# Two expert branches recomputed with features on partitions and 512 tokens as columns

## The chip, the cores and the metric

The kernel runs on one NeuronCore of a Trainium2 chip. The metric is the device time of the whole program in microseconds (us). Engines: PE is TensorE (matmul), DVE is VectorE, ACT is ScalarE, POOL is GpSimd, SP is SyncE, which here only issues DMAs.

## The reference, cut to what matters

x has 2 batches of 2048 tokens with 256 features. Two layers follow each other; each computes `x = x + s * silu(...)`, with s an attention output. The change lies in the feed-forward part of layer 0, whose two branches (forward and inverse, 8 experts of rank 64 each) are

```
xV = einsum('btd,kdr->btkr', Q_side, V)           # 8 experts x 64 per branch
yW = einsum('btd,kdr->btkr', K_side, W)
prod = xV * cumsum(yW, axis=1)
weights = softmax(gelu(Q_side @ router_w1.T + b1) @ router_w2.T + b2 + expert_bias)
out = einsum('btkr,kdr->btd', prod * weights[..., None], U) + weights @ b
out = out / n_valid                                # 1, 2, 3, ... along the sequence
g = silu((fwd + alpha * inv) @ W_O.T)
x1 = x + (attention @ W_o.T + b_o + xn) * g
```

Both branches together have 2 * 8 * 64 = 1024 columns per token. Float32 precision is kept by splitting operands into a high part of a shorter type (fp32r) and the rest, and by three products (high*high, high*rest, rest*high).

## The kernel before, in words

The program is a chain of phases with a barrier between them: weights, projection of layer 0, full attention, combination with the experts (`phase_combine_experts`, here called the stage), then projection, banded attention and combination of layer 1. The folded weights AQ, BK (256 x 1024), UO (1024 x 256) and bO are made once in the weights phase; the softmaxed router weights, already divided by n_valid, lie in SBUF as `logits`, tokens on partitions. The projection has left the transposed normed input (xT) and its running sum (cT) in DRAM, high part and rest.

The stage works on 32 tiles of 128 tokens, four to a chunk of 512 tokens, chunks in the order batch 0, batch 1, batch 0, ... For each tile, tokens lie on partitions:

- `front` (L1743 to L1759): ps_xv[128 x 1024] = xT.T @ AQ and ps_cy[128 x 1024] = cT.T @ BK, each 2 x 6 matmuls (`split_matmul`, L66 to L73) of 512 columns.
- ACT copies ps_xv to SBUF (L1822), DVE multiplies with ps_cy (L1861), POOL multiplies by the router weights (L1898).
- `turn` (L1761 to L1777): TensorE transposes the tile of attention outputs (2 transposes), of router weights (1) and of the weighted products (8, into ps_pt). ACT copies the high parts (L1811 to L1816), DVE makes the rests (L1849 to L1854).
- `out` (L1779 to L1789): 6 matmuls of 256 columns with o0, 24 with UO, and the plain float32 product with bO (2 records in the trace).
- ACT takes the tanh (L1828), DVE makes the gate (`gate_steps`, L1941 and L1943), POOL multiplies and adds to x (`residual`, L1950 and L1952).

The order on TensorE is turn(n), front(n + 1), out(n). So the router and split steps of one tile have a whole front of the next to finish in. SP loads chunk by chunk, two buffers (one a batch); one semaphore per buffer counts all 14 loads of a chunk (turned operands, x, xn and four pieces of attention), and front waits for the whole of it (L1747). The batches of 8 tiles run in a hardware loop of 3 turns with one more copy behind it.

Of the kernel before, what the change touches and what calls it, by code (L numbers as in the profile page):

```python
# [23 lines left out]
F32 = mybir.dt.float32  # L24
# [1621 lines left out]
def load_att(sp, S, att, loaded, i, u):  # L1646

    for hg in range(NG2):
        slot = (u * NG2 + hg) * NCH + i + 1
        sp.dma_start(att[:, u, :, hg * G * C:(hg + 1) * G * C],  # L1650
                     S["att"][ds(slot, 1)].rearrange("o (a p) c -> p (o a) c", p=P)).then_inc(loaded, DMA)


def store_and_load(sp, passed, x1_done, stored, x_io, out_dram, load):

    def store(i, u):
        wait_apart(sp, x1_done, 2 + TILES_BODY * i + TT * (u + 1), passed)
        sp.dma_start(out_dram[u, ds(i * CH, CH), :].rearrange("(t p) d -> p t d", p=P), x_io[:, u]
                     ).then_inc(stored[u], DMA)

    load(0, 0)
    load(0, 1)
    with sp.Fori(0, NCH - 1) as i:
        for u in range(2):
            store(i, u)
            wait_apart(sp, stored[u], DMA * (i + 1), passed)
            load(i + 1, u)
    for u in range(2):
        store(NCH - 1, u)
    for u in range(2):  # L1670
        wait_apart(sp, stored[u], DMA * NCH, passed)


def phase_combine_experts(nc, W, S, x_dram, out_dram):


    with ExitStack() as ctx:
        n_ = Names(nc, ctx, "c0")
        x_io = n_.sb("x_io", [P, 2, TT, D])
        xn = n_.sb("xn", [P, 2, TT, D])  # L1680
        att = n_.sb("att", [P, 2, TT, D])
        xT = n_.sb("xT", [P, 2, 2, DK, CH], F32R)
        cT = n_.sb("cT", [P, 2, 2, DK, CH], F32R)
        xv = n_.sb("xv", [P, 2 * KR])
        prod = n_.sb("prod", [P, 2 * KR])
        wprod = n_.sb("wprod", [P, 2 * KR])
        pT = n_.sb("pT", [P, 2, 2 * KR], F32R)
        aT = n_.sb("aT", [P, 2, D], F32R)
        wT = n_.sb("wT", [2 * E, P])
        wtile = n_.sb("wtile", [P, TILES_BODY, 2 * E])  # L1690
        sums = n_.sb("sums", [P, 2, D])
        eg = n_.sb("eg", [P, D])
# [3 lines left out]
        ps_pt = n_.ps("ps_pt", 2 * CH)  # L1696
        ps_out = n_.ps("ps_out", CH)
        ps_m = n_.ps("ps_m", CH)

        passed = n_.sem("passed")  # L1700
        loaded = [n_.sem(f"loaded{u}") for u in range(2)]
        stored = [n_.sem(f"stored{u}") for u in range(2)]
        xv_ready = n_.sem("xv_ready")
        cy_ready = n_.sem("cy_ready")
        xv_copied = n_.sem("xv_copied")
        prod_done = n_.sem("prod_done")
        wprod_done = n_.sem("wprod_done")
        m_ready = n_.sem("m_ready")
        pt_ready = n_.sem("pt_ready")
        high = n_.sem("high")  # L1710
        low = n_.sem("low")
# [5 lines left out]
        wtile_done = n_.sem("wtile_done")  # L1717
# [4 lines left out]
        n_loads = 4 * DK + 2 + NG2  # L1722

        order = [(u, t) for u in range(2) for t in range(TT)]

        @block.sync
        def _(sp):
            def load(i, u):
                tok = ds(i * CH, CH)
                for part in range(2):  # L1730
                    for k in range(DK):
                        sp.dma_start(f32(xT[:, u, part, k, :]), S["xT"][u, part, k, :, tok]).then_inc(loaded[u], DMA)
                        sp.dma_start(f32(cT[:, u, part, k, :]), S["cT"][u, part, k, :, tok]).then_inc(loaded[u], DMA)
                rows = lambda x: x[u, tok, :].rearrange("(t p) d -> p t d", p=P)
                sp.dma_start(x_io[:, u], rows(x_dram)).then_inc(loaded[u], DMA)
                sp.dma_start(xn[:, u], rows(S["xn"])).then_inc(loaded[u], DMA)
                load_att(sp, S, att, loaded[u], i, u)

            store_and_load(sp, passed, x1_done, stored, x_io, out_dram, load)
# [555 lines left out]
```

## Time and profile before

| | us |
|---|---|
| median of 3 runs | 2621.84 (2611.28 to 2631.97) |
| the profiled execution, device time | 2636.41 |
| its span, first to last instruction | 2634.8 |
| PE busy | 2305.5 (88% of the span) |
| DVE, ACT, POOL busy | 1831.5, 1466.2, 442.8 |

The span is what lies between the first and the last instruction of the profiled execution; 1.6 us lie around it. Busy times are of the whole program; the stage in question is one part of it, from about 1716 us to 2099 us after the start of the span. PEld is the load of the stationary operand, which can run beside the matmul before it; its start times tell well how fast TensorE moves on, since the ends of matmuls are modelled.

### The profile page before, as it was taken

To read this page: it belongs to the slowest core of one execution; us is meant where nothing else is said; L and a number is where in the kernel's file an instruction comes from. 1 tells how busy PE (TensorE), PEld (TensorE's weight loads), DVE (VectorE), ACT (ScalarE), POOL (GpSimd) and SP (SyncE) were. 2 spreads that over 40 slices of the span, in tenths; PEclk is the share of its full clock that TensorE was granted. 3 is DMA by queue.
4 is the path that set the end of the run, shared out by engine and by line. 5 is a ranking of instruction groups with operands and counts; after the bars stand their busy time and mean duration, and the time that the engine had idled before them with its cause. 6 is when DMAs were issued, how large, how long until landed. Compare 5 with 4: busy or idle time off the path is not lost. (4 is left out here: it accounts for less than half of the span.)

```text
span 2634.8 us, 45348 instructions
## 1 busy us (share of the span) xinstructions
PE 2305.5 (88%) x15192; PEld 1296.4 (49%) x15192; DVE 1831.5 (70%) x3165; ACT 1466.2 (56%) x2211; POOL 442.8 (17%) x647
## 2 busy tenths in 40 slices
PE   4678499999999999999999999769999775799988
PEld 2456133333333333333333333258888664566568
DVE  2654789999999999999999999113333364768836
ACT  2343067777777777777777777712222231346543
POOL 0000000000000000000000000023333300346545
PEclk9799589999999999999999999979999987658799
DMA  3786900220400404004022000033323089856465
GB/s 116 240 274 236 132 3 5 43 29 7 65 3 19 53 5 64 8 11 61 3 43 31 7 17 3 7 112 83 109 77 114 33 299 306 147 120 155 110 174 161
DMA packets 204953, 229.59 MB, mean 87 GB/s; under 512 B 72576, under 2 KB 143104, under 8 KB 200896
## 3 DMA queue, kind: packets, MB, share of 16 engines
q1 hardware_dynamic: 191920, 208.63, 31.9%
q10 hardware_dynamic: 7152, 13.84, 2.8%
q0 software_dynamic: 5728, 5.00, 0.8%
q8 instruction: 107, 1.75, 0.3%
q14 instruction: 46, 0.38, 0.1%
HBM read 129.28 MB, written 96.73 MB: 86 GB/s over the span
## 5 line engine op out<-in xcount | busy, mean ns | idle before, releaser
L930 DVE TENSOR_REDUCE a_maxes<-a_ps_a 128x2 f32<-128x1024 f32 x1024 | 1202.7, 1221 | 117.6 <-PE a_ps_a L1043 112.7
L994 ACT ACTIVATE a_prob<-a_ps_s 128x512 f32<-128x512 f32 (+1 forms) x1376 | 1035.5, 804 | 372.8 <-PE a_ps_s L1069 366.8
L1069 PE MATMUL a_ps_s<-a_Q,a_K 50*128 50x512 f32 x2048 | 593.7, 453 | 91.2 <-ACT a_prob L994 89.5
L1043 PE MATMUL a_ps_a<-a_K,a_Q 48*128 48x512 f32 x2048 | 552.9, 455 | 31.6 <-DMA a_Q<-s_halves 16.9
L1081 PE MATMUL a_ps_o<-a_prob,a_V 128*32 128x512 f32 x4096 | 548.1, 607 | 0.1
L1069 PEld LDWEIGHTS a_ps_s<-a_Q,a_K 50*128 50x128 f32 x2048 | 279.6, 185 | 507.5 <-ACT a_prob L994 455.4
L1043 PEld LDWEIGHTS a_ps_a<-a_K,a_Q 48*128 48x128 f32 x2048 | 247.5, 190 | 231.6 <-issue 103.5
L888 POOL DMA_DIRECT2D a_Q<-a_m_parts x128 | 64.3, 502 | 1291.8 <-DVE a_m_parts L922 1288.1
L1412 DVE CUSTOM_DVE_ANT_0 a_scratch<-a_ps_a,k_mask 128x256 f32<-128x256 f32 (+1 forms) x512 | 178.6, 412 | 71.9 <-PE a_ps_a L1525 71.6
L1470 ACT ACTIVATE a_prob<-a_ps_s 128x512 f32<-128x512 f32 (+1 forms) x256 | 136.1, 583 | 155.3 <-PE a_ps_s L1561 153.8
L1525 PE MATMUL a_ps_a<-a_K,a_Q 48*128 48x256 f32 (+1 forms) x512 | 137.2, 404 | 35.2 <-DMA a_Q<-s_halves 34.3
L1081 PEld LDWEIGHTS a_ps_o<-a_prob,a_V 128*32 128x32 f32 x4096 | 80.7, 108 | 150.1 <-issue 97.3
L1861 DVE TENSOR_TENSOR c_prod<-c_ps_cy,c_xv 128x1024 f32<-128x1024 f32 x32 | 39.2, 1225 | 160.9 <-issue 103.3
L1561 PE MATMUL a_ps_s<-a_Q,a_K 50*128 50x256 f32 (+2 forms) x576 | 124.0, 363 | 4.6 <-DMA a_Q<-a_m_parts 4.6
L71 PE MATMUL c_ps_xv<-k_AQ,c_xT 128*128 128x512 f32 x384 | 101.0, 413 | 23.7 <-DMA c_att<-s_att 23.7
L1561 PEld LDWEIGHTS a_ps_s<-a_Q,a_K 50*128 50x128 f32 x576 | 94.9, 246 | 52.3 <-ACT a_prob L1470 33.4
L1525 PEld LDWEIGHTS a_ps_a<-a_K,a_Q 48*128 48x128 f32 x512 | 98.9, 261 | 42.0 <-DMA a_Q<-s_halves 35.4
L1828 ACT ACTIVATE c_eg<-c_ps_out 128x256 f32<-128x256 f32 x32 | 12.3, 383 | 188.7 <-PE c_ps_out L1788 188.7
L71 PE MATMUL p_ps_qk<-p_xT,k_qkv 128*128 128x512 f32 x384 | 100.9, 418 | 10.4 <-DVE p_xT L490 5.6
L1391 POOL TENSOR_SCALAR_AFFINE_SELECT a_prob<-a_prob 128x512 f32<-128x512 f32 (+1 forms) x128 | 79.5, 621 | 177.8 <-ACT a_prob L1470 177.0
L1576 PE MATMUL a_ps_o<-a_prob,a_V 128*32 128x192 f32 (+2 forms) x1408 | 103.1, 401 | 0.0
L586 ACT ACTIVATE p_parts<-p_ps_qk,k_bqk 128x512 fp32r<-128x512 f32 x64 | 43.8, 687 | 93.1 <-PE p_ps_qk L71 53.1
(175 smaller groups left out, 2394.7 us busy)
## 6 DMA issues: line engine op xcount, KB each, us to landing
s_halves<-p_parts SPq DMA_DIRECT2D x64, 512.0 KB, 5.0
s_xT<-p_xT SPq DMA_DIRECT2D x64, 256.0 KB, 4.3
s_v<-p_v_out SPq DMA_DIRECT2D x64, 256.0 KB, 3.8
c_xT<-s_xT SPq DMA_DIRECT2D x64, 256.0 KB, 5.0
a_K<-s_halves SPq DMA_DIRECT2D x63, 256.0 KB, 7.2
a_Q<-s_halves SPq DMA_DIRECT2D x186, 64.0 KB, 10.5
s_cT<-p_cT SPq DMA_DIRECT2D x32, 256.0 KB, 3.5
a_V<-s_v SPq DMA_DIRECT2D x32, 256.0 KB, 3.2
```

The lines of the kernel that those rows point to most:

```text
L71: last = nc.tensor.matmul(out, stationary(s, k), moving(m, k), start=start and n == 0, stop=stop and n == len(passes) - 1, skip_group_chec ...
L930: nc.vector.tensor_reduce(maxes[:, :, slot, qt, kc], ps_a[:, o:o + 2 * CH].rearrange("p (z k) -> p z k", z=2), AX.X, ALU.max).then_inc(a_d ...
L994: nc.scalar.activation(prob[:, ring:ring + len(t), :].rearrange("p r q -> p (r q)"), ps_s[:, bank:bank + len(t) * CH], ACT.Exp, scale=scal ...
L1043: last = nc.tensor.matmul(ps_a[:, o + side * CH:o + (side + 1) * CH], Q[rows, q0:q0 + P], K[rows, k0:k0 + CH], start=True, stop=True)
L1069: last = nc.tensor.matmul(ps_s[:, bank + x * CH:bank + (x + 1) * CH], K[rows, k0:k0 + P], Q[rows, q0:q0 + CH], start=True, stop=True)
L1081: last = nc.tensor.matmul(ps_o[h * VW:(h + 1) * VW, :], V[:, kt, h * VW:(h + 1) * VW], prob[:, ring, :], start=(kt == 0), stop=(kt == KT - 1),
L1391: pool.affine_select(out=left, in_=left, compare_op=ALU.is_ge, fill=0.0, base=first, pattern=[[0, G], [1, P - first]], channel_multiplier= ...
L1412: nc.vector.tensor_tensor_reduce(scratch[:, (2 * a + x) % (2 * BANKS), first:last], ps_a[:, o + first:o + last], W["mask"][:, first:last], ...
L1470: nc.scalar.activation(prob[:, s % RING, side, :, first:last], scores[:, :, first:last], ACT.Exp, scale=scale).then_inc(exp_done, 1)
L1525: last_mm = nc.tensor.matmul(ps_a[:, o + first:o + last], Q[rows, query(g, slot, (qt0 + x) * P):][:, 0:P], K[rows, base + lo:base + hi], s ...
L1561: last_mm = nc.tensor.matmul(ps_s[:, c0:c0 + q1 - q0], K[rows, k0:k0 + P], Q[rows, query(g, slot, q0):][:, 0:q1 - q0], start=True, stop=Tr ...
L1576: last_mm = nc.tensor.matmul(ps_o[h * VW:(h + 1) * VW, o + q0:o + q1], V[:, g % 2, kt, h * VW:(h + 1) * VW], prob[:, s % RING, h % 2, h // ...
```

## The change

The stage turns its layout. For a chunk of 512 tokens, feature tile ft (0 to 7, 128 of the 1024 columns each) is computed with features on partitions: stationary AQ[:, ft], moving xT with 512 token columns, again 6 matmuls for ps_xv and 6 for ps_cy. The product then already has the layout that the UO product needs as its stationary operand, so the 8 transposes a tile, and ps_pt, go. DVE makes both multiplications (ps_xv times router weights, then ps_cy times that), ACT copies the high part, POOL makes the rest. The router weights now are needed along partitions: TensorE transposes them once a chunk (4 transposes), ACT copies them to wT, SP stores them to a new DRAM tensor `w` and loads them back with each row repeated over 64 partitions (wb, 2 MB a chunk, in two halves of 4 feature tiles). All out products of a chunk come after its 8 feature tiles, first the four with o0, then the four with bO and UO. Loads have semaphores of their own; xn, att and wb have one buffer. Python unrolls the loop over chunks. RT, w2, qkv0, b1 and b2 are freed behind the projection of layer 0 so that the new tiles fit.

```diff
-        xn = n_.sb("xn", [P, 2, TT, D])
-        att = n_.sb("att", [P, 2, TT, D])
+        xn = n_.sb("xn", [P, TT, D])
+        att = n_.sb("att", [P, TT, D])
...
-        xv = n_.sb("xv", [P, 2 * KR])
-        prod = n_.sb("prod", [P, 2 * KR])
-        wprod = n_.sb("wprod", [P, 2 * KR])
-        pT = n_.sb("pT", [P, 2, 2 * KR], F32R)
...
+        wb = n_.sb("wb", [P, FT, CH])
+        wx = n_.sb("wx", [P, 2, CH])
+        wp = n_.sb("wp", [P, 2, CH])
+        pT = n_.sb("pT", [P, 2, FT, CH], F32R)
+        aT = n_.sb("aT", [P, TT, 2, D], F32R)
+        wT = n_.sb("wT", [2 * E, 2, CH])
...
+            def load_weights(c, half):
+
+                src = S["w"].rearrange("(f z) b t -> z f b t", z=2)
+                for z in range(2):
+                    each = src[z, half * HALF_FT:(half + 1) * HALF_FT, batch(c), tokens(c)]
+                    sp.dma_start(wb[z * R:(z + 1) * R, half * HALF_FT:(half + 1) * HALF_FT, :],
+                                 each.unsqueeze(0).broadcast_to([R, HALF_FT, CH])).then_inc(wb_loaded[half], DMA)
+
+            load_turned(0)
+            store_weights(0)
+            wait_apart(sp, w_stored, DMA, passed)
+            load_weights(0, 0)
+            load_weights(0, 1)
+            load_attention(0)
+            load_normed(0)
+            load_rows(0)
+            load_turned(1)
+            load_rows(1)
+            for c in range(CHUNKS):
+                more = c + 1 < CHUNKS
+                if c > 0:
+                    wait_apart(sp, cy_ready, FT * c, passed)
+                    if more:
+                        load_turned(c + 1)
+                    wait_apart(sp, m_ready, TT * c, passed)
+                    load_attention(c)
+                    wait_apart(sp, bias_done, TT * c, passed)
+                    load_normed(c)
+                if more:
+                    store_weights(c + 1)
+                if c > 0:
+                    store_rows(c - 1)
+                if c > 0 and more:
+                    wait_apart(sp, stored[(c - 1) % 2], DMA * ((c - 1) // 2 + 1), passed)
+                    load_rows(c + 1)
+                if more:
+                    wait_apart(sp, w_stored, DMA * (c + 2), passed)
+                    for half in range(2):
+                        wait_apart(sp, mul1, FT * c + HALF_FT * (half + 1), passed)
+                        load_weights(c + 1, half)
...
+            def front(c, ft):
+                n, o = FT * c + ft, (ft % 2) * CH
+                if ft == 0:
+                    pe.wait_ge(kt_loaded[c % 2], 4 * DK * DMA * (c // 2 + 1))
+                if n > 1:
+                    pe.wait_ge(mul1, n - 1)
+                split_matmul(nc, ps_xv[:, o:o + CH], lambda s, k: W["AQ"][:, s, k, ft * P:(ft + 1) * P],
+                             lambda s, k: xT[:, c % 2, s, k, :], DK, True, True).then_inc(xv_ready, 1)
+                if n > 1:
+                    pe.wait_ge(mul2, n - 1)
+                split_matmul(nc, ps_cy[:, o:o + CH], lambda s, k: W["BK"][:, s, k, ft * P:(ft + 1) * P],
+                             lambda s, k: cT[:, c % 2, s, k, :], DK, True, True).then_inc(cy_ready, 1)
...
+            def out_attention(c, t):
                 if t == 0:
...
+                    pe.wait_ge(a_low, TT * (c + 1))
...
+            turn_weights(0)
+            for c in range(CHUNKS):
+                for ft in range(FT):
+                    front(c, ft)
+                    if ft == W_AT and c + 1 < CHUNKS:
+                        turn_weights(c + 1)
+                    if ft >= FT - TT:
+                        turn(c, ft - FT + TT)
+                for t in range(TT):
+                    out_attention(c, t)
+                for t in range(TT):
+                    out_experts(c, t)
...
+            copy_weights(0)
+            for c in range(CHUNKS):
+                for ft in range(FT):
+                    if ft >= FT - TT:
+                        attention_high(c, ft - FT + TT)
+                    product_high(c, ft)
+                    if ft == W_AT and c + 1 < CHUNKS:
+                        copy_weights(c + 1)
+                for t in range(TT):
+                    gate_tanh(c, t)
...
+            for c in range(CHUNKS):
+                for ft in range(FT):
+                    multiply_weights(c, ft)
+                    if ft > FT - TT:
+                        attention_low(c, ft - FT + TT - 1)
+                    multiply_sums(c, ft)
+                attention_low(c, TT - 1)
+                for t in range(TT):
+                    n = TT * c + t
+                    gate_steps(nc, dve, n, sums[:, n % 2], sums[:, n % 2], (bias_done, n + 1), gate[:, n % 2],
+                               th[:], s_region(t), g_region(t), exp_done, step, out_read, x1_done)
...
+            def product_low(c, ft):
+                pool.wait_ge(p_high, FT * c + ft + 1)
+                pool.tensor_tensor(pT[:, 1, ft, :], wp[:, ft % 2, :], f32(pT[:, 0, ft, :]), ALU.subtract
+                                   ).then_inc(p_low, 1)
```

`multiply_weights(c, ft)` waits for xv_ready, at ft 0 and 4 for its half of wb, and writes wx; `multiply_sums(c, ft)` waits for cy_ready and, from the third on, for POOL's rest of two feature tiles before, and writes wp. `out_experts(c, t)` is the bO product followed by 24 matmuls with UO for one tile of 128 tokens; for t = 0 it waits before each feature tile for p_low. `copy_weights`, `attention_high` and `product_high` are the ACT copies, `attention_low` the DVE rest of the attention outputs.

## Rows read from the trace of the kernel before

**Rows 1.** Windows view, a stretch inside the stage: busy us, clock, DMA share, GB/s.

```profile
1820.00:1860.00 40.00, 40.00 (x244) 34.24 (x243) 13.27 (x23) 10.74 (x24) 16.43 (x17) 1.00 0.37 105
```

**Rows 2.** Timeline, one tile inside the stage: start us, us, engine, line, op.

```profile
1843.87 0.29 PEld L1788 LDWEIGHTS c_ps_out<-k_bO,c_wT 16*128 16x128 f32 x2
...
1844.50 0.20 PEld L1768 LDWEIGHTS c_ps_m<-k_ident,c_att 128*128 128x128 f32 x2 [0.33 <-issue]
1844.50 0.44 PE L1768 MATMUL c_ps_m<-k_ident,c_att 128*128 128x128 f32 x2
...
1844.78 0.90 PEld L1776 LDWEIGHTS c_ps_pt<-k_ident,c_wprod 128*128 128x128 f32 x8
...
1845.14 0.39 ACT L1811 ACTIVATE c_aT<-c_ps_m 128x256 fp32r<-128x256 f32 x1 [0.16 <-PE c_ps_m L1770]
...
1845.65 2.62 PEld L71 LDWEIGHTS c_ps_xv<-k_AQ,c_xT 128*128 128x128 f32 x12
...
1845.71 0.42 DVE L1849 TENSOR_TENSOR c_aT<-c_ps_m,c_aT 128x256 fp32r<-128x256 f32 x1
...
1848.32 2.76 PEld L71 LDWEIGHTS c_ps_cy<-k_BK,c_cT 128*128 128x128 f32 x12
...
1851.12 0.90 PEld L71 LDWEIGHTS c_ps_out<-k_o,c_aT 128*128 128x128 f32 x6
1851.35 0.88 PE L71 MATMUL c_ps_out<-k_o,c_aT 128*128 128x256 f32 x6
1851.60 1.23 DVE L1861 TENSOR_TENSOR c_prod<-c_ps_cy,c_xv 128x1024 f32<-128x1024 f32 x1 [4.13 <-issue]
1851.94 2.88 PEld L71 LDWEIGHTS c_ps_out<-k_UO,c_pT 128*128 128x128 f32 x24
...
1854.95 0.29 PEld L1788 LDWEIGHTS c_ps_out<-k_bO,c_wT 16*128 16x128 f32 x2
```

**Rows 3.** Groups of instructions in the stage: busy us, mean ns; then idle before.

```profile
L1898 POOL TENSOR_TENSOR c_wprod<-c_prod,c_wtile 128x1024 f32<-128x1024 f32 x32 | 60.9, 1905 | 158.6 <-DVE c_prod L1861 158.6
L1852 DVE TENSOR_TENSOR c_pT<-c_ps_pt,c_pT 128x512 fp32r<-128x512 f32 x64 | 41.2, 686 | 4.7 <-ACT c_pT L1815 3.0
...
L1776 PEld LDWEIGHTS c_ps_pt<-k_ident,c_wprod 128*128 128x128 f32 x256 | 28.9, 140 | 3.9 <-POOL c_wprod L1898 3.3
...
L1950 POOL TENSOR_TENSOR c_sums<-c_sums,c_gate 128x256 f32<-128x256 f32 x32 | 23.7, 742 | 69.9 <-DVE c_gate L1943 69.9
```

**Rows 4.** Timeline of the stage's last tile.

```profile
2089.94 1.29 DVE L1852 TENSOR_TENSOR c_pT<-c_ps_pt,c_pT 128x512 fp32r<-128x512 f32 x2
...
2091.38 0.95 PE L71 MATMUL c_ps_out<-k_o,c_aT 128*128 128x256 f32 x6 [1.70 <-DVE c_pT L1852]
...
2095.09 0.29 PEld L1788 LDWEIGHTS c_ps_out<-k_bO,c_wT 16*128 16x128 f32 x2
```

**Rows 5.** Timeline of the stage's start.

```profile
1720.49 0.43 SPq L1733 DMA_DIRECT2D c_cT<-s_cT  x1
...
1731.69 4.77 PEld L71 LDWEIGHTS c_ps_xv<-k_AQ,c_xT 128*128 128x128 f32 x12 [23.96 <-DMA c_att<-s_att]
...
1739.79 0.38 PEld L1768 LDWEIGHTS c_ps_m<-k_ident,c_att 128*128 128x128 f32 x2
...
1744.39 4.16 PEld L71 LDWEIGHTS c_ps_xv<-k_AQ,c_xT 128*128 128x128 f32 x12
```

**Rows 6.** DMA issues, 1715 to 1735 us: KB each, median us from issue to landing.

```profile
c_cT<-s_cT SPq DMA_DIRECT2D x8, 256.0 KB, 5.3
...
c_att<-s_att SPq DMA_DIRECT2D x5, 128.0 KB, 7.1
```

**Rows 7.** The issues of att by SP: ns min/median/max of the issuing instruction.

```profile
L1650 SPq DMA_DIRECT2D c_att<-s_att x32: 430/1336/3714, 1722.0 to 2029.8; - x32
```

**Rows 8.** Timeline, projection of layer 0, warm TensorE after a stop.

```profile
169.57 2.63 PEld L71 LDWEIGHTS p_ps_h<-p_xT,k_RT 128*128 128x128 f32 x12 [1.84 <-ACT p_gelu L595]
```

**Rows 9.** DMA queues, first 60 us: packets, MB, share of 16 engines.

```profile
q10 hardware_dynamic: 2112, 0.53, 5.0%
```

More of the change, by code:

```diff
@@ L1643, in router_weights_vector, with batch, tokens @@
     nc.vector.tensor_tensor(logits, logits, each(inv), ALU.mult).then_inc(step, 1)
[L1646 to L1671, printed above, removed]
-def phase_combine_experts(nc, W, S, x_dram, out_dram):
+def phase_combine_experts(nc, W, S, x_dram, out_dram):
+    CHUNKS = 2 * NCH
+    FT = 2 * KR // P
+    HALF_FT = FT // 2
+    W_AT = 2
+    def batch(c):
+        return c % 2
+    def tokens(c):
+        return slice((c // 2) * CH, (c // 2 + 1) * CH)
     with ExitStack() as ctx:
@@ new lines, in turn @@
+            def turn(c, t):
+                if t == 0:
+                    pe.wait_ge(att_loaded, NG2 * DMA * (c + 1))
+                    if c > 0:
+                        pe.wait_ge(out_read, TT * c)
+                if t > 1:
+                    pe.wait_ge(a_low, TT * c + t - 1)
+                for k in range(DK):
+                    last = nc.tensor.transpose(s_region(t)[:, k * P:(k + 1) * P], att[:, t, k * P:(k + 1) * P],
+                                               W["ident"][:])
+                last.then_inc(m_ready, 1)
@@ L1877, in _, with multiply_weights @@
[L1877 to L1880 removed]
+            def multiply_weights(c, ft):
+                n, o = FT * c + ft, (ft % 2) * CH
+                dve.wait_ge(xv_ready, n + 1)
+                if ft % HALF_FT == 0:
+                    dve.wait_ge(wb_loaded[ft // HALF_FT], 2 * DMA * (c + 1))
+                if n > 1:
+                    dve.wait_ge(mul2, n - 1)
+                nc.vector.tensor_tensor(wx[:, ft % 2, :], ps_xv[:, o:o + CH], wb[:, ft, :], ALU.mult
+                                        ).then_inc(mul1, 1)
@@ L1929, in _, with add @@
-            router_weights(0, 0, None)
-            bias(0, 0)
-            weighted(0, 0)
-            with pool.Fori(0, NCH - 1) as i:
-                body(i, True)
-            body(NCH - 1, False)
+                pool.tensor_tensor(sums[:, n % 2], xn[:, t], W["bo"][:, 0], ALU.add).then_inc(bias_done, 1)
+            def add(c, t):
+                n = TT * c + t
+                if t == 0:
+                    wait_apart(pool, x_loaded[c % 2], DMA * (c // 2 + 1), passed)
+                residual(pool, n, x_io[:, c % 2, t], sums[:, n % 2], gate[:, n % 2], out_read, step, mixed, x1_done,
+                         0)
@@ L1937, in gate_steps @@
+            pool.sem_inc(x1_done, 2)
+            for c in range(CHUNKS):
+                for ft in range(FT):
+                    product_low(c, ft)
+                    if ft in (3, 5):
+                        bias(c, ft // 2 - 1)
+                for t in range(TT):
+                    add(c, t)
+                    if t + 2 < TT:
+                        bias(c, t + 2)
 def gate_steps(nc, dve, n, s_sum, bias, bias_ready, gate, half_tanh, ps_s, ps_g, exp_done, step, out_read, x1_done):
```

303 lines of the change are left out of this document (120 added, 183 removed).

## The prediction

> **What bounds the kernel now.** The chain of waits at the end of the page names only the last few per cent, so I read the stage itself. First the windows view: inside the stage TensorE is busy in 40.00 of 40 us at the full clock, 2.4 GHz, while DVE has 13.27, ACT 10.74, POOL 16.43, and the DMA engines are busy 0.37 of the time [rows 1]. Then the timeline of one tile: the loads of stationary operands show where the 11.08 us of a tile go (1843.87 to 1854.95) [rows 2]. The steps between the starts of its groups are 0.63 for bO, 0.28 for the three transposes of attention and router weights, 0.87 for the eight transposes of the weighted product, 2.67 for xv, 2.80 for cy, 0.82 for o0, 3.01 for UO. They add to 11.08, and the same tile repeats unchanged. So the stage is bound by TensorE's own list; a microsecond taken from DVE, ACT or POOL buys nothing, one taken from TensorE's list counts, and so does each new stop of it. Last come the stage's two ends. At the start TensorE stands 23.96 us, the last part of it for the attention pieces [rows 5]. In steady units the stage starts late: bO of the last tile starts at 2095.09 [rows 4], with its 0.63 the end is 2095.72, and 32 x 11.08 = 354.6 before that is 1741.2, though the first matmul was at 1731.69. The first tile lost 9.5 us to a cold clock and to the chain of its own product.
>
> **What goes, per chunk of four tiles.** The 256 transposes into ps_pt [rows 3]: 4 x 0.87 = 3.48 us. Matmuls and stationary loads of xv, cy, o0, UO and bO are as many and as wide as before; only which operand stands still is turned. TensorE's list for a chunk becomes 4 x 11.08 - 3.48 = 40.84 us. The four router transposes are now together and once a chunk, which is the same number. DVE loses a 128x1024 product a tile and gains two 128x512 ones a feature tile; ACT's 1024-column copy goes.
>
> **What comes: a stop at the end of the front.** Before, a whole front of 5.47 us lay between the turn of a tile and its out. Now out_attention follows the last turn at once and waits for the rest of that very transpose. With zero at the start of that transpose: it ends at 0.44; ACT starts about 0.1 later and takes 0.39, to 0.92. DVE is meanwhile in multiply_sums of feature tile 7; before, the product started 0.25 after the next group's matmul (1851.60 against 1851.35) [rows 2], and one such instruction of 512 columns takes 0.69 [rows 3], so it is free at 0.94. Then attention_low, 0.42, to about 1.4. In the last tile, where there was no front to hide it either, TensorE started 0.15 after DVE ended (2089.94 + 1.29, 2091.38) [rows 4]. So o0 starts at 1.6 instead of 0.2: a stop of 1.4 us a chunk. Bounds: 0 if something I overlook lets it through, 1.9 for the stop of the last tile (1.70 in its row) and a little. A chunk takes 40.84 + 1.4 = 42.24 against 44.32, a gain of 2.08; over 8 chunks **16.6 us**.
>
> **What stays hidden.** A feature tile takes TensorE 5.47/2 = 2.73 us. DVE has 2 x 0.69 and at most a 0.42 in it, 1.8 us. POOL's rest of 512 columns lies between 0.95 (half of 1905 ns for 1024) and 1.48 (twice 742 for 256) [rows 3]; I take 1.2, and with a bias of 0.74 beside it 1.9. The rest of feature tile 7 is due 21 UO matmuls into out_experts, some 6 us after the stop. In the out phase a tile takes TensorE 3.64, tanh and gate some 1.5 on ACT and DVE, POOL 2.2. SP now waits at seven places a chunk, and what queues behind them is always next chunk's: half 0 of wb is asked for after feature tile 3 and needed about 32 us later (four feature tiles, the stop, 17.8 us of out products), half 1 likewise; att and xn are asked for at the end of the previous front and during its out phase, and needed 25 us and 10 us later. The traffic of 6 MB in 42 us is 143 GB/s against 105 [rows 1]. If that cover were gone, each late microsecond of wb would count. The unrolled code and the freed tiles I cost at nothing, from -1 to +3 us, since no row shows either.
>
> **The start.** TensorE waits for xT and cT alone: the last of those issues is at 1720.49 [rows 5] and lands after 5.3 [rows 6], at 1725.8. Two feature tiles are 24 matmuls; cold they took 8.1 (1731.69 to 1739.79) [rows 5], so they are done at 1733.9. The third needs multiply_weights of the first, and so wb: the store of wT is issued by 1721.0 and landed by 1726.3, two issues of between 0.43 and 1.34 each [rows 7] end by 1728.0, and the load lands 5.3 to 7.1 later [rows 6], 1733.3 to 1735.1; I take 1734.2. With 0.69 of DVE and 0.1 TensorE goes on at 1735.0, warm, since a stop of 1.84 cost no clock in the projection (12 loads in 2.63) [rows 8]. Taking off the 5.47 that is done, the steady start is 1729.5 against 1741.2: **11.7 us**. Bounds 6 (wb lands like a slow one of small packets: the queue that made the broadcast of the biases moved 0.53 MB in 0.05 x 16 x 60 = 48 engine-us, 177 GB/s on 16 engines, so 1 MB takes 5.9 us [rows 9], and att comes late too) and 13 (wb never waited for). Attention is due at 1743.6 and lands at about 1742, so it doesn't count.
>
> Sum: 16.6 + 11.7 = 28.3 us off the profiled execution's 2636.41, 2608.1; the median of the runs shown lies 14.6 lower, and 2621.84 - 28.3 gives **2593.5**.
>
> The same load of wb is where the Trainium skill speaks against the change: "SBUF — State Buffer", section "Door 1: The DMA port swizzle", says that a transfer onto 64 partitions reaches half of the ports (196 against 328 GB/s at 1 MiB) and that two of them side by side don't add up. By that rule, as an estimate from the page, the half of wb that the start waits for would land some 2 us later, and the sum would be 26 instead of 28; in the steady chunks it would change nothing, as 2 MB at 196 GB/s are 10.7 us of 42. No row here has a DMA of 64 partitions.
>
> **Rivals.**
> 1. The pipeline breaks at places that I count as smooth: small stops between feature tiles of the kind that rows with [0.33 <-issue] show behind a plain float32 product [rows 2]. One such gap more per out tile (bO now stands before UO) is 32 x 0.33 = 10.6 us, giving 2604. For it: bO and UO now alternate with a wait. Against: the gap is already in the 0.63 of bO.
> 2. The stop at the end of each front throttles the clock. The first tile shows that: after its stop of 3.3 us for POOL [rows 3] the loads of xv at 1744.39 took 4.16 instead of 2.62 [rows 2, 5]. At 1.5 a chunk it gives back 12 us: 2605.5. Against it stands the 1.84 stop without loss [rows 8].
> 3. It doesn't gain at the start: wb comes at the slow bound. 2599.
> 4. Slower: POOL becomes the bound of the front. It decides from 2.73 us a product_low; the whole gain is gone at 28.3/64 = 0.44 more, 3.2 us, and at 3.5 the time is 2643. For it: POOL's instructions are the slowest a column here, and the longest wait of DVE hangs on them (p_low). Against: even the upper bound is 1.48.
> 5. The change doesn't do what it says: TensorE's 8 transposes were free under other work. Rows 2 speak against it, since the steps between loads add up with them in. 2610.
>
> **How the numbers follow.** Forecast 0.60; rival 1 0.12, rival 2 0.09, rival 3 0.11, rival 4 0.04, rival 5 0.04. Low end: stop of 0.5 instead of 1.4 and the best start, 28.3 + 7.2 + 1.3 + 1 = 38, 2584. High end: slow start and the small stops together, 28.3 - 5.7 - 10.6 = 12, 2610. A measurement of this kernel can tell about 1% from no change, 26.2 us, that is 2595.6; the forecast lies just beyond it, so its 0.60 parts into 0.48 faster and 0.12 same, and of the rivals only 0.02 is faster. Faster 0.50, same 0.45, slower 0.05.
>
> **What the profile after would show.** No ps_pt rows; loads of xv and cy in groups of 6 at the old pitch of 0.23; once a chunk a stop of 1.4 us before o0, ended by DVE's aT; a chunk every 42.2 us; POOL's rest of 1.2 us; the first matmul near 1726 and a stop of about 1 us before the third feature tile, ended by DVE's wx. I am wrong if the chunk is off 42.2 by more than half a microsecond, if DVE waits for wb in a later chunk, or if the clock inside the stage falls under 1.

## The result, and the profile after

The changed kernel takes 2606.03 us (median of 20 runs, 2587.88 to 2622.93) against 2620.6 (20 runs, 2607.7 to 2649.73) for the kernel before, taken beside it: a ratio of 0.994, 95% interval 0.9912 to 0.9969. That is 14.6 us faster, half of the 28.3 that were forecast. The profiled execution took 2610.0 us instead of 2636.4, 26.4 less.

Rows of the changed kernel's page (busy us of each engine; then the granted clock in 40 slices of the span, 9 for 0.9 and more):

```profile
span 2608.4 us, 44405 instructions
...
PE 2278.8 (87%) x14936; PEld 1263.6 (48%) x14936; DVE 1837.0 (70%) x3197; ACT 1443.0 (55%) x2155; POOL 462.2 (18%) x671
...
PEclk9799589999999999999999999969999987589689
```

PE has 26.7 us less to do and 256 matmuls fewer, the transposes. A stretch inside the stage in the windows view, the same as [rows 1]:

```profile
1820.00:1860.00 40.00, 39.07 (x222) 32.76 (x223) 15.20 (x28) 8.21 (x16) 17.63 (x18) 1.00 0.54 150
```

TensorE is still the bound, at the full clock, but it now stands 0.93 us of the 40; ACT has less, DVE and POOL a little more, and the DMA engines are busy 0.54 of the time instead of 0.37.

The timeline of one chunk, loads of stationary operands, to be held against the tile in [rows 2] (start us, us):

```profile
2034.11 1.23 PEld L71 LDWEIGHTS c_ps_xv<-c_xT,k_AQ 128*128 128x128 f32 x6
2035.39 1.36 PEld L71 LDWEIGHTS c_ps_cy<-c_cT,k_BK 128*128 128x128 f32 x6
2036.79 1.36 PEld L71 LDWEIGHTS c_ps_xv<-c_xT,k_AQ 128*128 128x128 f32 x6
...
2039.59 1.36 PEld L71 LDWEIGHTS c_ps_xv<-c_xT,k_AQ 128*128 128x128 f32 x6
...
2057.04 0.37 PEld L1829 LDWEIGHTS c_ps_s<-k_ident,c_att 128*128 128x128 f32 x2
2058.59 2.88 PEld L71 LDWEIGHTS c_ps_s<-k_o,c_aT 128*128 128x128 f32 x24 [1.17 <-DVE c_aT L1928]
2061.60 0.29 PEld L1845 LDWEIGHTS c_ps_g<-k_bO,c_wT 16*128 16x128 f32 x2
2062.23 2.91 PEld L1851 LDWEIGHTS c_ps_g<-k_UO,c_pT 128*128 128x128 f32 x24 [0.33 <-issue]
2065.28 0.29 PEld L1845 LDWEIGHTS c_ps_g<-k_bO,c_wT 16*128 16x128 f32 x2
```

A feature tile that follows another takes 2.80 us (2036.79 to 2039.59), bO and UO of one token tile 3.63 to 3.68 (3.64 before), and the only stop of more than 0.33 us is the 1.17 us before o0. What ends it is to be seen in the timeline of all engines at that place:

```profile
2057.27 0.38 PE L1829 MATMUL c_ps_s<-k_ident,c_att 128*128 128x128 f32 x2
2057.47 0.69 DVE L1923 TENSOR_TENSOR c_wp<-c_ps_cy,c_wx 128x512 f32<-128x512 f32 x1 [0.38 <-PE c_ps_cy L71]
2057.69 0.38 ACT L1885 ACTIVATE c_aT<-c_ps_s 128x256 fp32r<-128x256 f32 x1 [1.89 <-PE c_ps_s L1829]
2058.11 0.42 DVE L1928 TENSOR_TENSOR c_aT<-c_ps_s,c_aT 128x256 fp32r<-128x256 f32 x1
```

The last transpose, its copy on ACT (done at 2058.07), its rest on DVE and then o0 at 2058.59 stand one behind the other. DVE's product of feature tile 7 ends at 2058.16, so it holds the rest back just as long as the copy does.

The start of the stage, which answers to [rows 5]:

```profile
1724.63 0.33 SPq L1724 DMA_DIRECT2D c_xT<-s_xT  x1
...
1733.89 2.20 PEld L71 LDWEIGHTS c_ps_xv<-c_xT,k_AQ 128*128 128x128 f32 x6 [8.69 <-DMA c_cT<-s_cT]
...
1734.10 3.69 SPq L1756 DMA_DIRECT2D c_wb<-s_w  x4
...
1743.00 0.69 DVE L1914 TENSOR_TENSOR c_wx<-c_ps_xv,c_wb 128x512 f32<-128x512 f32 x1 [25.55 <-DMA c_wb<-s_w]
...
1743.75 1.23 PEld L71 LDWEIGHTS c_ps_xv<-c_xT,k_AQ 128*128 128x128 f32 x6 [2.18 <-DVE c_wx L1914]
1745.02 1.36 PEld L71 LDWEIGHTS c_ps_cy<-c_cT,k_BK 128*128 128x128 f32 x6
```

Where did the time go? Cut by phases, the two profiled executions differ as follows (from the first load of the stage to the first instruction of the next projection, DVE's memset).

| | before | after | difference |
|---|---|---|---|
| up to the stage's first load | 1715.9 | 1724.6 | +8.7 |
| the stage | 387.9 | 359.7 | -28.2 |
| behind it | 531.0 | 524.1 | -6.9 |

The stage gave what was forecast. What lies before and behind it has the same code and still moved by 8.7 and 6.9 us. Ahead of the stage two things add up: the last 50 us of the full attention took 11.7 us longer, all that lies before them 3.0 less. The windows view of five microseconds out of those 50 shows what goes with the 11.7. Before:

```profile
1690.00:1695.00 5.00, 3.88 (x25) 1.27 (x25) 0.00 (x0) 4.18 (x6) 0.00 (x0) 1.00 0.01 2
```

After:

```profile
1690.00:1695.00 5.00, 4.74 (x15) 1.33 (x15) 0.00 (x0) 2.33 (x4) 0.00 (x0) 0.50 0.00 2
```

The granted clock is 0.50 (1.2 GHz) and TensorE gets through 15 matmuls instead of 25. So three questions are left: is the stage's gain there in every execution, is each of its terms what I said, and is the clock in the attention chance or a price of the change.

### The profile page after: what moved, and what is told of

The parts are those of the page before. It is cut to its first block and busy times, and to the rows that moved or that the text cites. A ratio compares the mean times of both kernels' runs of the same rounds, so it can differ in the third digit from the quotient of the medians.

```text
span 2608.4 us, 44405 instructions
## 1 busy us (share of the span) xinstructions
PE 2278.8 (87%) x14936; PEld 1263.6 (48%) x14936; DVE 1837.0 (70%) x3197; ACT 1443.0 (55%) x2155; POOL 462.2 (18%) x671
## 5 line engine op out<-in xcount | busy, mean ns | idle before, releaser
L1043 PE MATMUL a_ps_a<-a_K,a_Q 48*128 48x512 f32 x2048 | 552.1, 454 | 30.6 <-DMA a_Q<-s_halves 16.6
L1081 PE MATMUL a_ps_o<-a_prob,a_V 128*32 128x512 f32 x4096 | 554.8, 614 | 0.1
L1069 PEld LDWEIGHTS a_ps_s<-a_Q,a_K 50*128 50x128 f32 x2048 | 280.5, 187 | 509.4 <-ACT a_prob L994 459.3
L1043 PEld LDWEIGHTS a_ps_a<-a_K,a_Q 48*128 48x128 f32 x2048 | 246.7, 190 | 232.4 <-issue 103.4
L1525 PE MATMUL a_ps_a<-a_K,a_Q 48*128 48x256 f32 (+1 forms) x512 | 130.7, 385 | 35.7 <-DMA a_Q<-s_halves 34.9
L1561 PE MATMUL a_ps_s<-a_Q,a_K 50*128 50x256 f32 (+2 forms) x576 | 116.1, 345 | 8.4 <-DMA a_Q<-a_m_parts 8.4
L1561 PEld LDWEIGHTS a_ps_s<-a_Q,a_K 50*128 50x128 f32 x576 | 88.0, 229 | 52.7 <-ACT a_prob L1470 32.0
L1525 PEld LDWEIGHTS a_ps_a<-a_K,a_Q 48*128 48x128 f32 x512 | 92.6, 243 | 43.0 <-DMA a_Q<-s_halves 36.2
L71 PE MATMUL c_ps_xv<-c_xT,k_AQ 128*128 128x512 f32 x384 | 104.0, 406 | 9.9 <-DMA c_cT<-s_cT 8.2
L1947 POOL TENSOR_TENSOR c_pT<-c_wp,c_pT 128x512 fp32r<-128x512 f32 x64 | 82.9, 1295 | 115.2 <-ACT c_pT L1881 115.1
L1980 DVE TENSOR_TENSOR c_sums<-c_ps_s,c_sums 128x256 f32<-128x256 f32 x32 | 13.6, 424 | 127.2 <-ACT c_th L1892 127.2
L71 PE MATMUL c_ps_cy<-c_cT,k_BK 128*128 128x512 f32 x384 | 101.0, 398 | 0.0
L1851 PE MATMUL c_ps_g<-k_UO,c_pT 128*128 128x256 f32 x768 | 98.8, 284 | 0.0
```

What stands on the lines that cost most here:

```text
L71: last = nc.tensor.matmul(out, stationary(s, k), moving(m, k), start=start and n == 0, stop=stop and n == len(passes) - 1, skip_group_chec ...
L1043: last = nc.tensor.matmul(ps_a[:, o + side * CH:o + (side + 1) * CH], Q[rows, q0:q0 + P], K[rows, k0:k0 + CH], start=True, stop=True)
L1069: last = nc.tensor.matmul(ps_s[:, bank + x * CH:bank + (x + 1) * CH], K[rows, k0:k0 + P], Q[rows, q0:q0 + CH], start=True, stop=True)
L1081: last = nc.tensor.matmul(ps_o[h * VW:(h + 1) * VW, :], V[:, kt, h * VW:(h + 1) * VW], prob[:, ring, :], start=(kt == 0), stop=(kt == KT - 1),
L1525: last_mm = nc.tensor.matmul(ps_a[:, o + first:o + last], Q[rows, query(g, slot, (qt0 + x) * P):][:, 0:P], K[rows, base + lo:base + hi], s ...
L1561: last_mm = nc.tensor.matmul(ps_s[:, c0:c0 + q1 - q0], K[rows, k0:k0 + P], Q[rows, query(g, slot, q0):][:, 0:q1 - q0], start=True, stop=Tr ...
```

## The experiments

**1 and 2. The stage without the phases that scatter.** Both kernels keep the weights phase, the first projection and the stage; both attentions and layer 1 are left out, and the attention outputs are read from x (in `load_attention` the slot index loses its + 1 for that).

```diff
-            phase_attend_full(nc, W, S)
-            phase_combine_experts(nc, W, S, I["x"], S["x1"])
-        phase_project(nc, W, S, S["x1"], 1)
-        phase_attend_band(nc, W, S)
-        phase_combine_lora(nc, W, S, S["x1"], out)
+            S["att"] = I["x"].rearrange("b (s t) d -> (b s t d)", s=16).rearrange("(o t c) -> o t c", t=CH, c=G * C)
+            phase_combine_experts(nc, W, S, I["x"], out)
```

With the stage of before:

> Weights, projection of layer 0 and the stage as before; both attentions and all of layer 1 are left out (the stage reads x in place of the attention outputs and writes the output). My theory (the stage gains 28 us, and what the whole program shows less than that is scatter of the phases around it): this is the base line; the stage lasts 387.9 us from its first load to the first instruction of the next phase in the whole program, 380 from first load to last store here, and the kernel some 620 us. Rival (the stage itself gains only some 15 us in most executions, and the profiled one was lucky): the same base line.

With the turned stage:

> The same cut with the turned stage. My theory: 28 us below the cut kernel with the stage of before, within 3, in the medians as in the profiles, since nothing that scatters is left. Rival (the stage gains only half in most executions): 12 to 18 us below, with executions spread between.

Measured, five runs each on one chip: 658.82 us (657.16 to 661.21) and 632.04 (629.44 to 635.01). The difference is 26.8 us, within the 28 give or take 3 that were expected, and the two sets of five lie 22 us apart at their nearest. The stage's gain is in every execution, not in a lucky profile; the rival is out. The base line itself was 39 us longer than the 620 expected: the stage's first load starts at 270.2 us, not at 240.

**3. The transposes back, and nothing else.** Whole program.

```diff
-                for k in range(DK):
+                for k in 5 * list(range(DK)):
                     last = nc.tensor.transpose(s_region(t)[:, k * P:(k + 1) * P], att[:, t, k * P:(k + 1) * P],
```

> The turned stage, whole program, with each transpose of attention outputs made five times, so that the 8 transposes a tile that the change removed are back on TensorE's list and nothing else is. My theory: a chunk lasts 42.3 + 4 x 0.87 = 45.8 us, the stage is 27 to 28 us longer than after. Rival (the transposes were hidden under other work): a chunk within 0.5 us of 42.3.

Measured: 2633.55 us (12 runs) against 2631.6 for the kernel before on that chip, 1.0019 (0.9986 to 1.0053). The timeline of TensorE in this kernel:

```profile
1769.64 3.12 PE L71 MATMUL c_ps_s<-k_o,c_aT 128*128 128x256 f32 x24 [0.93 <-DVE c_aT L1928]
...
1815.43 3.09 PE L71 MATMUL c_ps_s<-k_o,c_aT 128*128 128x256 f32 x24 [0.93 <-DVE c_aT L1928]
```

From o0 to o0 there are 45.79 us, 3.5 more than in the changed kernel, and the stage is 390.3 us long, 30.6 more than the changed kernel's, where 27 to 28 were expected; 28 are the transposes (8 x 3.5), the rest lies in its start, as told under 9 and 10. With as many transposes as before the turned stage is worth nothing. The transposes are the whole of the net gain, though not because nothing else changed: the eight new stops cost about what the shorter start gives.

**4. The stop before o0 taken away.** The transposes of attention outputs, their copies and rests come one feature tile earlier (on PE, ACT and DVE alike).

```diff
-                    if ft >= FT - TT:
-                        turn(c, ft - FT + TT)
+                    if FT - TT - 1 <= ft < FT - 1:
+                        turn(c, ft - FT + TT + 1)
```

> The turned stage with the transposes of attention outputs (and their copy and rest) one feature tile earlier, so that the eighth feature tile lies between the last of them and the o0 products. My theory: the stop of 1.1 us a chunk before o0 goes, a chunk lasts 41.2 us, the stage is 8 to 9 us shorter, less up to 2 us at the start where the attention pieces may be late. Rival (the stop moves, since DVE is then late for feature tile 7 or PSUM comes free later): a chunk stays at 42.3.

Its timeline, loads:

```profile
1760.95 2.92 PEld L71 LDWEIGHTS c_ps_s<-k_o,c_aT 128*128 128x128 f32 x24 [0.15 <-DVE c_aT L1928]
1802.08 2.92 PEld L71 LDWEIGHTS c_ps_s<-k_o,c_aT 128*128 128x128 f32 x24 [0.15 <-DVE c_aT L1928]
```

The stop is 0.15 instead of 1.17, a chunk 41.13 us, 1.15 less, as expected. The stage is 353.6, 6.1 shorter than the changed kernel's in the profile, at the low end of the expected 8 to 9 less up to 2: eight chunks give 9.2, and the start takes 3.1 of them back, only 0.42 of it by late attention pieces; the rest is the stop before the third feature tile, told under 9 and 10. The whole program took 2607.85 us (11 runs) against 2631.6 before: 0.9908 (0.9876 to 0.994).

**5 and 6. Is the clock in the attention the price of the freed tiles?** First the stage of before with the tiles freed as in the change (and nothing else of the change):

```diff
+            with ExitStack() as first_projection:
+                n1 = Names(nc, first_projection, "k1")
...
+                phase_weights(nc, W, I)
+                phase_project(nc, W, S, I["x"], 0)
```

> The stage as before, but RT, w2, qkv0, b1 and b2 freed behind the projection of layer 0, so that only the places of tiles in SBUF differ from the kernel before. My theory (the 13 us by which the medians of the whole program show less than the stage gained are the clock in phases that the change doesn't touch, which falls or not by chance): within 8 us of the kernel before, and the last 50 us of the full attention at 2.4 GHz or at 1.2 GHz by chance. Rival (the freed tiles change something in the attention): some 10 us slower than before, with 20 to 30 us at 1.2 GHz at the end of the attention as in the three profiles of kernels with the new places.

Then the kernel before, unchanged:

> The kernel before once more, for a second profile of it. My theory: the stage again lasts 387.9 us within half a microsecond, the phases around it differ from the first profile by several us, and the clock at the end of the attention is low for some of the time. Rival: full clock there again, as in the first profile of before.

Measured: 2623.81 us (12 runs) and 2622.06 (12 runs), against 2633.45 (23 runs) for the kernel before; ratios 0.9946 (0.992 to 0.9972) and 0.9946 (0.9914 to 0.9979). An exact copy lay half a per cent under its original, with an interval that leaves 1 out. So the moved tiles cost nothing that shows, and an interval of this comparison is too narrow by about half a per cent. The stage of the copy was 390.3 us, 2.4 longer than in the first profile: my half microsecond was too tight. In it the first load of a stationary operand comes 16.8 us behind the stage's first DMA instead of 15.8, and a tile takes 11.12 instead of 11.08 us. At the end of the attention the clock was low for 31 us in the first kernel. In the copy it was low for 3 us only: some of the time, as I expected, but closer to the rival's full clock.

**7. The repeated weights loaded twice** (in every chunk but the first, the second load behind the first; DVE waits for both). One execution, 2638.83 us.

```diff
-                for z in range(2):
+                for z in range(2) if c == 0 else (0, 1, None, 0, 1):
+                    if z is None:
+                        wait_apart(sp, wb_loaded[half], 4 * DMA * c, passed)
+                        continue
...
-                    dve.wait_ge(wb_loaded[ft // HALF_FT], 2 * DMA * (c + 1))
+                    dve.wait_ge(wb_loaded[ft // HALF_FT], 2 * DMA * (2 * c + 1))
```

> The turned stage with the repeated router weights loaded twice, one load after the other, in every chunk but the first: 8 MB a chunk instead of 6. My theory (the load is hidden): a chunk stays at 42.3 us, the DMA engines are busy some 0.7 to 0.9 of the stage. Rival (the rule on 64 partitions makes the load so slow that its cover is thin): DVE waits for wb in later chunks and a chunk is some us longer.

My expectation fell, and mostly not for the rival's reason. The stage took 396.5 us, with the DMA engines busy 0.67 of it (0.7 to 0.9 were expected). The starts of o0 in the second to the fifth chunk (the first was at 1752.11):

```profile
1809.77 2.91 PEld L71 LDWEIGHTS c_ps_s<-k_o,c_aT 128*128 128x128 f32 x24 [1.17 <-DVE c_aT L1931]
1854.49 2.88 PEld L71 LDWEIGHTS c_ps_s<-k_o,c_aT 128*128 128x128 f32 x24 [1.17 <-DVE c_aT L1931]
1903.42 2.88 PEld L71 LDWEIGHTS c_ps_s<-k_o,c_aT 128*128 128x128 f32 x24 [1.17 <-DVE c_aT L1931]
1949.68 2.88 PEld L71 LDWEIGHTS c_ps_s<-k_o,c_aT 128*128 128x128 f32 x24 [1.17 <-DVE c_aT L1931]
```

Chunks of 57.7, 44.7, 48.9 and 46.3 us, where the changed kernel has 42.3. Its view of waits (waited for, us in total, times, longest) and one row of SP's timeline name the reason:

```profile
PE c_ps_s L1832 <- DMA c_att<-s_att: 26.2, 6, 12.4
...
DVE c_wx L1917 <- DMA c_wb<-s_w: 31.2, 2, 26.2
```

```profile
1800.33 26.11 SPq L1759 DMA_DIRECT2D c_wb<-s_w  x8
```

DVE waited for wb only once after the start (5.0 us); TensorE waited six times for the attention pieces, 12.4 us of it in the second chunk, and there the clock also fell behind the stop. SP issues in order, and it spent 26 us on the two halves of wb, where it spends 9.8 in the changed kernel, as it now waited for each first load to land; att and the next turned operands came behind. In the changed kernel itself DVE waits for wb at the start and never again, so there the load is hidden; this run shows that what queues behind it is late first. As the edit adds both traffic and SP's waits, it doesn't tell their shares.

**8. POOL made slow.** Two more subtractions ahead of each rest, 1.04 us each. One execution, 2616.5 us.

```diff
+                for e in range(2):
+                    if 2 * (FT * c + ft) + e > 0:
+                        pool.wait_ge(extra, 2 * (FT * c + ft) + e)
+                    pool.tensor_tensor(again[:], wp[:, ft % 2, 0:384], f32(pT[:, 0, ft, 0:384]), ALU.subtract
+                                       ).then_inc(extra, 1)
```

> The turned stage with two more subtractions of 384 columns on POOL ahead of each product_low, some 1.0 us each, so that a feature tile takes POOL 3.3 us where TensorE takes 2.8. By my prediction's rival 4 as it stood (it decides from 2.73 us, and at 3.2 the gain of the stage is gone): a chunk 3.5 us longer, 45.8. What I now think, since POOL may lag into the out products, where it has little to do, and DVE only waits for the rest of two feature tiles before: less than 1.5 us a chunk, 42.3 to 43.8.

The starts of o0 in three of the eight chunks:

```profile
1804.69 4.43 PEld L71 LDWEIGHTS c_ps_s<-k_o,c_aT 128*128 128x128 f32 x24 [2.67 <-DVE c_aT L1930]
1849.99 2.88 PEld L71 LDWEIGHTS c_ps_s<-k_o,c_aT 128*128 128x128 f32 x24 [2.65 <-DVE c_aT L1930]
1893.81 4.29 PEld L71 LDWEIGHTS c_ps_s<-k_o,c_aT 128*128 128x128 f32 x24 [2.68 <-DVE c_aT L1930]
```

Chunks take 45.1 to 45.3 or 43.8 us, 44.6 in the mean, so a chunk became 2.3 us longer, more than the 1.5 that I then thought and less than the 3.5 of the prediction's rival. 43.8 is the price of POOL alone, 1.5 a chunk. The other 1.3 to 1.5 in the longer chunks go with the clock. The windows view behind two such stops:

```profile
1804.00:1809.00 5.00, 4.30 (x23) 4.30 (x24) 0.64 (x2) 0.63 (x1) 4.84 (x6) 0.66 0.82 157
...
1850.00:1855.00 5.00, 5.00 (x37) 4.53 (x38) 0.00 (x0) 0.27 (x1) 4.84 (x6) 1.00 0.78 163
```

After the stop of 2.67 us TensorE ran partly at 1.2 GHz (0.66 in the mean) and o0's 24 loads took 4.43 us instead of 2.88; after the next, as long, it didn't. Of the eight stops before o0, 2.65 to 3.63 us long, five were followed by slow loads, the first and then every second one. In the changed kernel eight stops of 1.17 us never were. So rival 2 of the prediction names something real, at stops about twice as long as those that the change makes before o0.

**9 and 10. Both kernels as equals.** An exact copy of before and one of the changed kernel, run side by side.

> The kernel before once more, to be compared with the next kernel instead of with the base runs, from which an exact copy lay 0.5% off in the last call. My theory (base runs and tried kernels differ by up to half a per cent whatever their code): again up to 0.5% off the base runs. Rival (the last one was an accident of a skewed sample): the interval holds 1.

> The changed kernel once more. My theory (the stage gives 27 us in every execution): the median 20 to 34 us below that of the copy of before in this call, and the stage in the profile 359.7 us within 2. Rival (part of the gain is lost elsewhere): 15 us or less below the copy.

Measured: 2624.31 us (12 runs) and 2604.58 (12 runs), 19.7 apart; against 23 runs of the kernel before (2628.1) they are 1.0002 (0.9967 to 1.0037) and 0.9917 (0.9887 to 0.9948). The offset of experiment 6 didn't come again: the interval holds 1, as the rival to my expectation had it. The distance of the two lies 0.3 under my 20 to 34, and above the 15 or less of its rival. The stages were 390.3 and 362.6 us long, 27.7 apart; 362.6 is 2.9 more than in the first profile of the changed kernel, where I had allowed 2. The place is the start, at the third feature tile of the copy:

```profile
1738.50 1.43 PEld L71 LDWEIGHTS c_ps_xv<-c_xT,k_AQ 128*128 128x128 f32 x6 [2.58 <-DVE c_wx L1914]
1740.03 2.47 PEld L71 LDWEIGHTS c_ps_cy<-c_cT,k_BK 128*128 128x128 f32 x6
```

The tile starts 20.5 us behind the first load of the stage (at 1718.00) instead of 19.1, and behind its stop of 2.58 us the six loads of cy took 2.47 us instead of the 1.36 that they took behind the stop of 2.18 us in the first profile; the granted clock from 1740 to 1743 us is 0.52. In eight profiles of the turned stage (the changed kernel, its copy, experiments 2 to 4, 7, 8 and 11) this stop was 2.18, 2.30, 2.30 and 2.32 us without slow loads behind it, and 2.49, 2.58, 2.81 and 3.11 with them. So the changed kernel has one stop, at its start, where rival 2 does come true in some executions; it costs about 1.5 us once.

**11 and 12. Can the start be shortened?** In the cut program, with the transposes early:

> The cut program (weights, projection and the stage alone, attention outputs read from x) with the attention outputs turned one feature tile earlier. The stop of 1.17 us before o0 shrinks to 0.15 eight times: 8 x 1.14 = 9.1 us below the cut kernel with the stage as changed (632.0), less what the start loses: 624 to 626. Rival (the start gives it back, since the attention pieces are late for the fourth feature tile): above 628.

and besides, the first store of the router weights issued by ACT:

```diff
             load_turned(0)
-            store_weights(0)
...
             copy_weights(0)
+            act.wait_ge(wt_copied, 1)
+            act.dma_start(S["w"][:, batch(0), tokens(0)], wT[:, 0, :]).then_inc(w_stored, DMA)
```

> As the kernel before it in this list, and the first store of the router weights is issued by ACT right behind its copy instead of by SP behind the eight loads of turned operands. My theory (the start waits for the chain store, load of wb): the store no longer queues behind 2 MB, wb comes some 3 us earlier, TensorE's stop before the third feature tile goes, 2 us less than without. Rival (the loads of the turned operands and wb share the same DMA engines, so that wb lands when it did): no difference.

Measured: 622.28 us (617.83 to 624.05) and 620.66 (619.92 to 623.85), five runs each, against 632.04 for the cut kernel with the stage as changed, which ran on another chip. The first is 9.8 us faster in the medians, more than the 6 to 8 expected, and 7.8 in the profiles (621.8 us of span against 629.6). One row of its start shows the small loss that was feared:

```profile
297.83 0.20 PEld L1829 LDWEIGHTS c_ps_s<-k_ident,c_att 128*128 128x128 f32 x2 [1.89 <-DMA c_att<-in_x]
```

In the second kernel:

```profile
286.72 0.69 DVE L1915 TENSOR_TENSOR c_wx<-c_ps_xv,c_wb 128x512 f32<-128x512 f32 x1 [18.33 <-DMA c_wb<-s_w]
...
288.81 1.36 PEld L71 LDWEIGHTS c_ps_xv<-c_xT,k_AQ 128*128 128x128 f32 x6
```

DVE starts 15.3 us after the stage's first load (at 271.45) instead of 18.4, and neither stop of TensorE is left in the start. The profiles differ by 2.9 us; the medians by 1.6, with sets that overlap, so the step is seen in the trace, and the times don't show it.

## Why the prediction was right, and where its terms were off

**The stage.** Forecast 28.3 us less; 28.2 in the pair of profiles, 26.8 in the cut kernels, 27.7 in the pair of copies. What its terms measured in the first pair:

| term | forecast | measured |
|---|---|---|
| eight transposes a tile, a chunk | 3.48 | 3.5 (experiment 3) |
| eight feature tiles on TensorE | 21.9 | 21.8 |
| o0, bO and UO of a chunk | 17.8 | 17.4 |
| four router and three attention transposes, up to the last one | 0.95 | 1.56 |
| last transpose to o0 | 1.6 | 1.54 (1.17 of it in the load row) |
| a chunk | 42.24 | 42.28 (o0 at 1763.06 and 1805.34) |
| POOL's rest of 512 columns | 1.2 | 1.295 |
| first load to first matmul | 9.9 | 9.3 |
| first load to third feature tile | 19.1 | 19.1 |
| start of the stage, gain | 11.7 | 11.9 (28.2 less 8 x 2.04) |

The rows of one chunk from which the middle of the table comes:

```profile
1763.06 2.91 PEld L71 LDWEIGHTS c_ps_s<-k_o,c_aT 128*128 128x128 f32 x24 [1.17 <-DVE c_aT L1928]
...
1780.43 1.23 PEld L71 LDWEIGHTS c_ps_xv<-c_xT,k_AQ 128*128 128x128 f32 x6
...
1788.71 0.54 PEld L1803 LDWEIGHTS c_ps_g<-k_ident,k_logits 128*16 128x16 f32 x4
...
1803.80 0.37 PEld L1829 LDWEIGHTS c_ps_s<-k_ident,c_att 128*128 128x128 f32 x2
1805.34 2.88 PEld L71 LDWEIGHTS c_ps_s<-k_o,c_aT 128*128 128x128 f32 x24 [1.17 <-DVE c_aT L1928]
```

The chunk came out to 0.04 us by errors that took each other out. The transposes now stand alone or in fours between other work, and the two of one token tile take a step of 0.34 us where the tile of before has 0.17: 0.6 more a chunk than I took. The out products are 0.5 shorter, since the o0 products of four tiles in one row take 3.01 to 3.04 us instead of 4 x 0.82, and the last UO gives way to xv after 2.81 instead of 3.01. A feature tile takes 2.80 where it follows another one (xv then steps 1.40 for six, like cy) and 2.68 behind a transpose or UO; I had 2.73 for all. The stop itself, that it would be there, between which instructions and what ends it, is as written.

At the start two errors cancelled also. The store of wT had landed a microsecond earlier than I took it (SP issues wb at 1734.10, 9.5 after the first load, where I had 10.4), and the first product came 8.9 us behind the issue of wb instead of 7.9, half of the 2 us that I had estimated from the page. TensorE was done with its two feature tiles a microsecond earlier too, so its stop before the third was 2.18 us and not about 1. The prediction named a rule that bears on the late wb: by the section "Door 1: The DMA port swizzle" of "SBUF — State Buffer" in the Trainium skill, 64 partitions reach half of the ports and 196 GB/s. The windows view of the changed kernel while wb was on its way (alone in the first row; the first load of att is issued at 1737.83):

```profile
1736.00:1738.00 2.00, 2.00 (x6) 1.51 (x6) 0.00 (x0) 0.00 (x0) 0.00 (x0) 0.50 0.99 181
1738.00:1740.00 2.00, 2.00 (x9) 1.58 (x8) 0.00 (x0) 0.00 (x0) 0.00 (x0) 0.79 0.92 155
```

The DMA engines are busy 0.92 to 0.99 of the time and move 155 to 181 GB/s. The loads of xT and cT onto 128 partitions, a few microseconds before (1728 to 1732 us), made 369 to 395 GB/s at a share of 1.00 to 1.04. So the trace agrees with the rule in size, though the repeated reads of the same rows could do the same, and no run here parts them.

**The whole program.** Measured 14.6 us in the first comparison, 19.7 in the copies. The mean over all executions that were taken side by side gives 18.6 (20 against 20) and 19.6 (35 against 12), together 19 with 5.6 either side. That is less than the 27 to 28 of the stage, and the measured 2606.0 lies near the slow end of the stated range, 2610. That it lies inside is partly luck: the range was made that wide for a slow start and for small stops, and neither came; what took some 8 us off the gain was in neither. The step of the prediction that was too simple is the one from the profile to the median: I took the sum over a single pair of executions as the answer, and gave the phases around the stage no term and no bound. Its sentence "A measurement of this kernel can tell about 1% from no change" was a fair guess of the noise, and the 14.6 us are less than that.

**What makes the scatter.** Single executions of the kernel before lie between 2601.8 and 2662.0 us. The table has two stretches of the ten profiles of the whole program. The first is the end of the full attention, from the last but two store of its outputs to the last; the low clock in it is added up from the windows view. The second is all that lies behind the stage, with its mean granted clock.

| kernel | tiles freed | end of attention, us | of it at 1.2 GHz, us | behind the stage, us | clock there |
|---|---|---|---|---|---|
| before | no | 49.7 | 0 | 531.0 | 0.77 |
| before, copy of experiment 6 | no | 51.2 | 3 | 510.7 | 0.83 |
| before, copy of experiment 9 | no | 51.2 | 3 | 529.9 | 0.79 |
| layout only | yes | 61.3 | 31 | 520.6 | 0.81 |
| changed | yes | 61.3 | 31 | 524.1 | 0.81 |
| changed, copy | yes | 54.9 | 14 | 531.7 | 0.78 |
| transposes back | yes | 61.4 | 31 | 516.0 | 0.82 |
| early transposes | yes | 56.3 | 17 | 531.1 | 0.78 |
| wb twice | yes | 51.2 | 3 | 527.7 | 0.78 |
| POOL slow | yes | 51.2 | 3 | 514.8 | 0.82 |

At the end of the attention each microsecond at 1.2 GHz goes with some 0.4 us more, up to 11.7. The larger part of the scatter is behind the stage: 21 us between the shortest and the longest, by and large the longer the lower the clock, and 510.7 and 531.0 are the same kernel.

That the clock at the end of the attention is chance is shown only in part: of seven profiles with the freed tiles five had it low for 14 us or more, of three without none. Kernels of both kinds of stage had it, and two with the freed tiles hadn't, so the freed tiles don't force it; whether they make it likelier stays open. A price of 6 us in the mean (56.8 against 50.7 us in the table) would explain most of the 8 us between the stage's gain and the program's. Against it speaks the layout-only kernel, whose mean lies 4.5 us under that of the copy measured with it. Experiment 4, whose mean lies 31 us under the kernel before (8 either side) where its stage alone gives 34 to 37, fits a price and none. Ten profiles can't settle it, and the cause of the 8 us stays open.

**The rivals.** Rival 1: its gap of 0.33 is there 32 times ([0.33 <-issue] before UO), but it had been in the 0.63 of bO as argued, and moved with it. Rival 2, the clock, didn't happen at the stops that it named, before o0, at 1.17 us each; it happened once at the start in the copy, behind 2.58 us, and in experiment 8 behind 2.66 us and more. Rival 3, the slow bound of wb, didn't happen at the start. Rival 4, POOL, didn't happen. In experiment 8 it proved right as a mechanism and too high in its price (1.5 us a chunk for POOL alone instead of 3.5); it forgot that POOL can run on into the out products. Rival 5 is out by experiment 3.

## What to carry to other kernels

Where one engine is busy without a gap, add up the steps between its own starts and strike out what the change removes; that gave a chunk to a tenth of a microsecond, though here partly by errors of half a microsecond that took each other out. Then look for the places where a producer and its consumer on that engine, once a stage apart, now stand next to each other: here one such place cost a third of what the removed work gave, and moving the producer one step up gave most of it back (experiments 4 and 11). And before a gain of one per cent is weighed, cut the program down to the part that changed, run an exact copy of the base beside the change, and average only over executions that were taken side by side.

## What the runs showed of the hardware

Behind stops of 2.49 to 3.63 us, in front of the third feature tile and before o0, TensorE's loads came at 1.2 GHz in nine cases (24 loads in 4.22 to 5.19 us instead of 2.88, six in 2.25 to 2.47 instead of 1.36) and in three of 2.65 us they didn't; behind stops of 1.17 us and of 2.18 to 2.32 us at these places they never did. At the end of the full attention the clock was at 1.2 GHz for 14 to 31 us in the middle of work in five of ten profiles, and for some 3 us in four more; in the stretches of 5 us ahead of it PE had been busy 3.7 to 4.7. Loads onto 64 partitions with each row repeated kept the DMA engines 0.92 to 0.99 busy at 155 to 181 GB/s, less than half of what loads of the same row length onto 128 partitions moved at nearly the same share.
